# Images behind the first k, first parts of Q and K read straight from PSUM, second parts on ScalarE

## The chip, the cores and the metric

The kernel is one program on one core of one Trainium2 chip. The metric is the device time of one execution in microseconds (us). Engines are called as the profile calls them: PE (TensorE), DVE (VectorE), ACT (ScalarE), POOL (GpSimd), SP (SyncE, which here only issues transfers).

## The reference, cut to what matters

Two layers over `x` (2 batches, 512 tokens, 128 channels). Layer 0 scales `x` by a softmax over the batch and puts it through a ternary-weight feed-forward. Layer 1 is an attention over words with one image key in front (causal, 16 heads of 8), then a second attention without a mask, layer norm, a router that picks one of 8 experts, the experts, and a second layer norm.

```
x  = x + ffn0(cond0(x))                        # quantised feed-forward
c  = proj(softmax(q k' / sqrt(8) + causal) v)  # keys: one image key, 512 words
a  = out(softmax(q2 k2' / sqrt(8)) v2)         # second attention, no mask
h  = layernorm(c + a);  x = x + layernorm(h + moe(h))
```

## The kernel before

There are four attention instances `a`: 0 and 1 are the causal attention of batch 0 and 1, 2 and 3 the second attention of batch 0 and 1. An instance has 64 `scores` steps (16 heads by 4 row tiles: the score block is made only for its row maximum), two `max` steps (8 heads each), 32 `attend` steps (transposed scores of one head and half of the keys on PE, Exp on ACT), 16 `values` steps, 4 `turn_back` and `normalise` steps.

Q and K go into the score matmuls as three bf16 parts each, stacked along the contraction. A part is made by rounding, the next by rounding what is left. In step `q`, ACT reads the PSUM bank `misc` into `Qf` (line 733), waits for that, and copies `Qf` into `Qp[:, 0]` (line 736); `k` does the same with `Kf` and `Kp` (739, 742). In step `q_parts` DVE subtracts (953, `qres`), copies the residue to bf16 (954) and subtracts once more (956); `k_parts` is the same (960, 961, 963). In step `send` SP writes the parts to DRAM, q first and then k (517, 523), and reads them back as stacks in three ranges of heads: heads 0 to 3, 4 to 7, 8 to 15, for each `Qs` (529) and then `Ks` (535). SP waits in order, so no stack is read before the last k part was made.

When a `max` step is done, PE transposes the negated maxima (`max_rows`, line 1266), ACT copies them (745) and SP writes them as two more rows of `Qs` (540, "the shift"). `attend` 0 of an instance waits for the shift of heads 0 to 7, `attend` 16 for that of heads 8 to 15 (line 1271).

The order of all work is a string, `MERGE`: every letter takes the next step of one chain, and each engine runs its own share of the steps in that one order. So one letter moved changes the order on every engine that has work in its step. The steps of the text: `U` is `images` (PE: four small fp32 products with the image vector and biases, 1159 to 1169, into `s0`, and a fused weight, 1173, into `s1`; DVE reads `s0`, 908 to 912; ACT reads `s1`, 721). `w` is the turning of weights and then `prepare` (888 to 903). `S` is `stacks` twice (POOL memsets) and then `load_small` (nine POOL-issued loads, 609). `f` and `g` hold the feed-forward and then q, k, v of instances 0 and 1. There is one PSUM bank `misc`; its users take turns, each waiting until the last one was read.

Of the kernel before, what the change touches and what calls it, by code (L numbers as in the profile page):

```python
# [24 lines left out]
HD = D // HEADS  # L25
# [20 lines left out]
MERGE = (  # L46
    "ffwTfgfffwgffffffffwugUgfgff44ggggggggvSV4S00000000000000000000000000000g0000000mi0000g000m000g0"
    "00f50A0AAE0A050Ag0AA500FAA00a00i000a1a1mM1aA1Am1A111a11A1A1A1A11aaI11AA1M1aa1A1A11a11IAA1a1A1A1A"
    "1M1a1a1A1aimA11AaIA11AmA11a1A1Ma11aa1B11aI11Ba11B1q1B11qB661Bq1BBbGb11B1B1i11B1bBm2b6NB2m22B22B2"
    "2bJB22b22b22B2b2B2B2bN2B22B2B2b2B2B2B2bbJ22B2B2b2B2BN2b2B2Bm2B2Jb2b2b2m222bb22JNb22Cb22CC22r22C7"  # L50
    "r27C27crcC2C22C22C2OcH22mcC3C33C3m3C3C3c33c3C3C3cC3C3cK33c3OC3C3c33KCC3c3C3C33C3c33c3C33C3C3Ocm3"
    "C3m3lC3C3c33c3C3cD33cDK33cO3D3DcK3D3dSD33c3DD33n33QQnddDdPD3D3dLD33Dn3D3DmnDQmdQexddDdPDnDeDnDDd"
    "QDLxddDDyzDLDPddDzDdDdDDyPxdddeLdedxszyxseyRezxRyzesyesxzxRRzyesxyzxesyRozexyoezxzyeyxezxyzexyey"
    "zxzzpoppy"
)


def program_order():
# [42 lines left out]
    for a in range(INST):  # L101
        chains["0123"[a]] = each("scores", a, HEADS * NT)
        chains["4567"[a]] = [(n, a, 0) for n in ("q_parts", "k_parts", "send")]
        chains["EFGH"[a]] = [("v_bias", a, 0)]
        chains["ABCD"[a]] = each("attend", a, UNITS)
        chains["abcd"[a]] = output(a)
        chains["MNOP"[a]] = each("keep", a, ROUNDS)
        chains["IJKL"[a]] = each("normalise", a, ROUNDS)
# [93 lines left out]
def two_layers(nc, A, out):  # L202
# [18 lines left out]
    with ctx:  # L221
# [189 lines left out]
        r2_ready = sem("r2_ready")  # L411
        qhi_ready, khi_ready = sem("qhi_ready"), sem("khi_ready")
        qrest_ready, krest_ready = sem("qrest_ready"), sem("krest_ready")
# [33 lines left out]
        def _(sp):  # L447
            for step, a, i in ORDER:
# [52 lines left out]
                if step == "send":  # L501
# [9 lines left out]
                    for n in range(PARTS):  # L511
                        if n == 0:
                            sp.wait_ge(qhi_ready, a + 1)
                        else:
                            sp.wait_ge(qrest_ready, a * (PARTS - 1) + n)
                        for copy in range(n, 2 * PARTS - 1, PARTS):
                            sp.dma_start(dram_q[copy], Qp[:, n, :]).then_inc(parts_q[a], 16)
                    for n in range(PARTS):
                        if n == 0:
                            sp.wait_ge(khi_ready, a + 1)  # L520
                        else:
                            sp.wait_ge(krest_ready, a * (PARTS - 1) + n)
                        sp.dma_start(dram_k[n], Kp[:, n, :]).then_inc(parts_k[a], 16)
# [125 lines left out]
        def _(act):  # L649
# [4 lines left out]
            for step, a, i in ORDER:  # L654
# [71 lines left out]
                if step == "q":  # L726
                    if a >= 1:
# [4 lines left out]
                    ps = take("misc", "q", a)  # L732
                    act.activation(Qf[:, b, :], ps[:, :], ACT.Identity, bias=cols5[:, 0:1] if a < 2 else bjoin[:, 0:1],
                                   scale=float(HD) ** -0.5).then_inc(free["misc"], 1)
                    act.wait_ge(free["misc"], filled("misc", "q", a))
                    act.activation(Qp[:, 0, :], Qf[:, b, :], ACT.Copy).then_inc(qhi_ready, 1)
                if step == "k":
                    ps = take("misc", "k", a)
                    act.activation(Kf[:, :], ps[:, :], ACT.Identity,
                                   bias=cols5[:, 1:2] if a < 2 else bjoin[:, 1:2]).then_inc(free["misc"], 1)  # L740
                    act.wait_ge(free["misc"], filled("misc", "k", a))
                    act.activation(Kp[:, 0, :], Kf[:, :], ACT.Copy).then_inc(khi_ready, 1)
                if step == "max_rows":
# [42 lines left out]
        def _(dve):  # L786
# [50 lines left out]
            for step, a, i in ORDER:  # L837
# [103 lines left out]
                if step == "x1":  # L941
# [7 lines left out]
                    last.then_inc(free["pv"], 1)  # L949
                if step == "q_parts":  # L950

                    dve.wait_ge(qhi_ready, a + 1)
                    then_wait(dve.tensor_tensor(qres[:, :], Qf[:, b, :], Qp[:, 0, :], ALU.subtract))
                    dve.tensor_copy(Qp[:, 1, :], qres[:, :]).then_inc(qrest_ready, 1)
                    dve.wait_ge(qrest_ready, a * (PARTS - 1) + 1)
                    dve.tensor_tensor(Qp[:, 2, :], qres[:, :], Qp[:, 1, :], ALU.subtract).then_inc(qrest_ready, 1)
                if step == "k_parts":

                    dve.wait_ge(khi_ready, a + 1)
                    then_wait(dve.tensor_tensor(kres[:, :], Kf[:, :], Kp[:, 0, :], ALU.subtract))  # L960
                    dve.tensor_copy(Kp[:, 1, :], kres[:, :]).then_inc(krest_ready, 1)
                    dve.wait_ge(krest_ready, a * (PARTS - 1) + 1)
# [145 lines left out]
        def _(pe):  # L1108
# [6 lines left out]
            for step, a, i in ORDER:  # L1115
# [166 lines left out]
                if step == "values":  # L1282

                    r, kb = i // NT, i % NT
                    u = kb // 2
                    half = 2 * (a * ROUNDS + r) + u
                    ps = put("pv", "values", a, r) if kb == 0 else place["pv"]
                    if kb % 2 == 0:
# [119 lines left out]
```

## Time and profile before

| what | value |
|---|---|
| median of 3 runs | 357.32 us (356.76 to 358.71) |
| profiled execution, its own time | 352.93 us |
| its span, first to last instruction | 351.1 us |
| PE busy | 293.8 us (84%) |
| DVE busy | 258.8 us (74%) |
| ACT busy | 168.8 us (48%) |
| POOL busy | 29.3 us (8%) |
| mean granted clock | 0.96 |

The busy times are of the profiled execution, and the shares are of its span. PE and DVE take turns as the engine that others wait for; ACT has room over the whole span.

### The profile page before, as it was taken

What the parts mean: (1) busy time and instruction counts of PE and PEld (TensorE: products, weight loads), DVE (VectorE), ACT (ScalarE), POOL (GpSimd) and SP (SyncE); (2) the same over time, 40 slices, a digit from 0 to 9 for tenths busy, and PEclk for the clock granted to TensorE, in tenths of its full rate; (3) what the DMA queues carried; (4) which work ended last, traced back from release to release, by engine and by line L of the source; (5) the groups of instructions that cost most, each with busy time, mean ns of one, the idle gap of its engine ahead of it and who ended that gap; (6) DMA issues with size and microseconds to landing.
All of it is one profiled execution on the core that took longest, in us unless ns stands there. A gap on an engine that the chain in (4) does not pass through costs nothing.

```text
span 351.1 us, 5408 instructions
## 1 busy us (share of the span) xinstructions
PE 293.8 (84%) x1862; PEld 149.9 (43%) x1888; DVE 258.8 (74%) x764; ACT 168.8 (48%) x246; POOL 29.3 (8%) x58
## 2 busy tenths in 40 slices
PE   0286945988889999789999999999899999899981
PEld 0134531345445554244342332334334457656760
DVE  6888687999767788979999788777813128558445
ACT  1864360055555686166286676674767621221110
POOL 3075000000000000600000000003000001001001
PEclk9999686599999999999999999999999999999997
DMA  6892157214620027800037500260000000001001
GB/s 191 177 194 57 27 158 175 58 34 141 166 57 3 2 74 200 156 7 2 2 86 189 130 1 0 56 187 2 0 2 2 0 2 1 2 0 30 0 2 31
DMA packets 14959, 22.83 MB, mean 65 GB/s; under 512 B 2190, under 2 KB 12306, under 8 KB 14164
## 3 DMA queue, kind: packets, MB, share of 16 engines
q1 hardware_dynamic: 14644, 22.21, 25.7%
q0 software_dynamic: 288, 0.28, 0.7%
q8 instruction: 15, 0.25, 0.3%
q14 instruction: 12, 0.10, 0.1%
HBM read 13.99 MB, written 4.72 MB: 53 GB/s over the span
## 4 chain that ended last, share of the span: by engine, by line
PE 43%; DVE 22%; issue 14%; DMA 10%; ACT 6%; SPq 2%; POOL 1%; POOLq 0%; another core or an unknown queue 0%; DVEq 0%; ACTq 0%
PE ps_pv L1294 10%; DVE mx L989 9%; PE ps_t L1276 7%; PE ps_s L1253 6%; DMA Qs<-nmT 6%; PE ps_s L1369 5%; PE ps_misc L1377 4%; ACT probs L770 3%; DVE shared L985 2%; DMA shared<-in_L_ffn_w_down 2%; DVE probs L919 1%; DVE shared L833 1%; DVE q L922 1%; DVE mx L985 1%; DMA Ks<-parts_k 1%
## 5 line engine op out<-in xcount | busy, mean ns | idle before, releaser
L770 ACT ACTIVATE probs<-ps_t 128x1024 f32<-128x1024 f32 (+2 forms) x128 | 105.6, 862 | 61.8 <-PE ps_t L1279 26.4
L989 DVE TENSOR_REDUCE mx<-ps_s 128x1 f32<-128x512 f32 x126 | 80.8, 685 | 13.7 <-PE ps_s L1253 12.4
L1253 PE MATMUL ps_s<-Ks,Qs 128*128 128x512 bf16 (+3 forms) x220 | 70.6, 347 | 11.0 <-DVE mx L985 2.8
L1276 PE MATMUL ps_t<-Qs,Ks 128*128 128x512 bf16 (+3 forms) x245 | 65.4, 338 | 6.2 <-DMA Qs<-nmT 3.8
L1294 PE MATMUL ps_pv<-probs,Vs 128*32 128x512 f32 (+3 forms) x512 | 55.5, 522 | 0.3 <-ACT probs L770 0.2
L985 DVE CUSTOM_DVE_ANT_0 shared<-ps_s,shared 128x128 bf16<-128x128 f32 (+3 forms) x106 | 45.6, 459 | 10.4 <-PE ps_s L1253 9.5
L1253 PEld LDWEIGHTS ps_s<-Ks,Qs 128*128 128x128 bf16 x232 | 21.7, 98 | 57.9 <-DVE mx L989 26.8
L1093 DVE SCALAR_TENSOR_TENSOR shared<-ps_misc,comb,shared 128x128 f32<-128x128 f32 x64 | 18.0, 343 | 31.1 <-PE ps_misc L1377 31.1
L1276 PEld LDWEIGHTS ps_t<-Qs,Ks 128*128 128x128 bf16 x256 | 23.5, 98 | 32.4 <-issue 10.7
L1377 PE MATMUL ps_misc<-Ks,shared 128*128 128x128 f32 x256 | 31.6, 277 | 4.2 <-DVE shared L1093 1.4
L1377 PEld LDWEIGHTS ps_misc<-Ks,shared 128*128 128x128 f32 x256 | 30.5, 192 | 9.6 <-issue 8.2
L1369 PE MATMUL ps_s<-Qf,Ks 128*128 128x512 f32 x64 | 30.3, 596 | 0.0
L756 ACT ACTIVATE shared<-ps_s,cols 128x512 f32<-128x512 f32 x16 | 11.0, 686 | 36.7 <-PE ps_s L1369 36.7
L1279 PE MATMUL ps_t<-causal_k,identb 128*128 128x128 bf16 x128 | 24.5, 219 | 0.3 <-issue 0.2
L1294 PEld LDWEIGHTS ps_pv<-probs,Vs 128*32 128x32 f32 x512 | 11.4, 108 | 21.2 <-issue 20.0
L639 POOL TENSOR_TENSOR shared<-shared,halves 128x4 f32<-128x4 f32 x4 | 4.1, 1036 | 193.7 <-DVE shared L823 193.7
L753 ACT ACTIVATE shared<-ps_pv 128x512 f32<-128x512 f32 x16 | 9.6, 597 | 12.1 <-PE ps_pv L1294 12.0
L1369 PEld LDWEIGHTS ps_s<-Qf,Ks 128*128 128x128 f32 x64 | 11.0, 191 | 9.5 <-issue 9.0
L1084 DVE TENSOR_SCALAR shared<-ps_s,cols 128x512 f32<-128x512 f32 x16 | 11.9, 744 | 3.4 <-PE ps_s L1369 3.4
L1279 PEld LDWEIGHTS ps_t<-causal_k,identb 128*128 128x128 bf16 x128 | 12.5, 98 | 3.2 <-issue 0.3
L985 DVE CUSTOM_DVE_ANT_0 shared<-ps_t,shared 128x512 bf16<-128x512 f32 (+1 forms) x22 | 13.0, 626 | 0.0
L633 POOL TENSOR_TENSOR Zimg<-Vimg,Pimg 128x288 f32<-128x288 f32 x4 | 2.7, 682 | 107.6 <-ACT Pimg L750 107.6
(244 smaller groups left out, 324.2 us busy)
## 6 DMA issues: line engine op xcount, KB each, us to landing
parts_q<-Qp SPq DMA_DIRECT2D x20, 128.0 KB, 1.9
Qs<-parts_q SPq DMA_DIRECT2D x24, 96.0 KB
Ks<-parts_k SPq DMA_DIRECT2D x24, 96.0 KB
Qs<-parts_q SPq DMA_DIRECT2D x12, 192.0 KB
Ks<-parts_k SPq DMA_DIRECT2D x12, 192.0 KB
Ks<-Qs SPq DMA_DIRECT2D x2, 1024.0 KB, 12.0
parts_k<-Kp SPq DMA_DIRECT2D x12, 128.0 KB, 1.8
Qs<-Qs SPq DMA_DIRECT2D x1, 1024.0 KB, 12.2
```

What stands on the lines that cost most here:

```text
L756: act.activation(hid[:, i % 2, 1, :], ps[:, :], ACT.Relu, bias=cols17[:, 2 * i + 1:2 * i + 2])\
L770: act.activation(probs[:, half % 2, j, 0:w], ps[:, 0:w], ACT.Exp).then_inc(free[f"t{i % 2}"], 1)
L985: last = dve.tensor_tensor_reduce(out=added[:, n % 2, 0:w], in0=ps[:, 0:w], in1=causal_q[:, S - w:], scale=1.0, scalar=LEAST, op0=ALU.add, ...
L989: last = dve.tensor_reduce(mx[:, b, t, h:h + 1], ps[:, 0:w], AX, ALU.max)
L1084: dve.tensor_scalar(hid[:, i % 2, 0, :], ps[:, :], cols17[:, 2 * i:2 * i + 1], 0.0, ALU.add, ALU.max).then_inc(free["s0"], 1)
L1093: last = dve.scalar_tensor_tensor(out=acc[:, a, t, :], in0=ps[:, t * D:(t + 1) * D], scalar=comb[:, a, t, i // 2, i % 2:i % 2 + 1], in1=ac ...
L1253: mm = pe.matmul(ps[:, 0:w], Qs[:, b, h, t * P:(t + 1) * P], Ks[:, b, h, 0:w], start=True, stop=True)
L1276: mm = pe.matmul(ps[:, col:col + w], Ks[:, b, h, kb * P:(kb + 1) * P], Qs[:, b, h, S - w:S], start=True, stop=(a >= 2))
L1279: mm = pe.matmul(ps[:, col:col + P], identb[:, :], causal_k[:, :], start=False, stop=True)
L1294: mm = pe.matmul(ps[j * HC:(j + 1) * HC, S - w:S], Vs[:, b, kb, r * GROUP + j, :], probs[:, half % 2, j, col:col + w], start=(kb == 0), st ...
L1369: pe.matmul(ps[:, :], W1[:, i, h * P:(h + 1) * P], X3T[:, a, :], start=True, stop=True)\
L1377: mm = pe.matmul(ps[:, t * D:(t + 1) * D], hid[:, i % 2, h, t * P:(t + 1) * P], W2[:, i, h, :], start=(h == 0), stop=(h == FH - 1))
```

## The change

1. `MERGE` is a new string. On PE and ACT `images` stands behind the first `q` and `k` of instance 0 (before: ahead of the last two `ffn_up` of batch 1); on DVE it stands between `q_lo` and `k_lo` of instance 0. `prepare` stands three steps earlier. `load_small` on POOL stands before the first `max_rows` (before: behind the fourth). In the attention stages `scores`, `attend` and `values` are merged anew: `attend` 16 of instance 0 stands behind `scores` 11 of instance 1 and ahead of `values` 4 (before: behind `scores` 16 and `values` 5).
2. `Qp[:, 0]` and `Kp[:, 0]` are read from PSUM with bias and scale, without a wait between the two reads. The bank is free after the second read.
3. The second parts are made by ACT (steps `q_mid`, `k_mid`) in place of DVE.
4. The subtractions are the DVE steps `q_res`, `k_res`, `q_lo`, `k_lo`, which other steps can stand between.
5. `values` 0 waits for the step that writes `Vs`.

```diff
-        chains["4567"[a]] = [(n, a, 0) for n in ("q_parts", "k_parts", "send")]
+        chains["4567"[a]] = [(n, a, 0) for n in ("q_res", "q_mid", "k_res", "k_mid", "q_lo", "k_lo", "send")]
...
                     act.activation(Qf[:, b, :], ps[:, :], ACT.Identity, bias=cols5[:, 0:1] if a < 2 else bjoin[:, 0:1],
+                                   scale=float(HD) ** -0.5)
+                    act.activation(Qp[:, 0, :], ps[:, :], ACT.Identity,
+                                   bias=cols5[:, 0:1] if a < 2 else bjoin[:, 0:1],
                                    scale=float(HD) ** -0.5).then_inc(free["misc"], 1)
-                    act.wait_ge(free["misc"], filled("misc", "q", a))
-                    act.activation(Qp[:, 0, :], Qf[:, b, :], ACT.Copy).then_inc(qhi_ready, 1)
...
+                if step == "q_mid":
+                    act.wait_ge(qres_ready, a + 1)
+                    act.activation(Qp[:, 1, :], qres[:, :], ACT.Copy).then_inc(qrest_ready, 1)
+                if step == "k_mid":
+                    act.wait_ge(kres_ready, a + 1)
+                    act.activation(Kp[:, 1, :], kres[:, :], ACT.Copy).then_inc(krest_ready, 1)
...
-                if step == "q_parts":
-
-                    dve.wait_ge(qhi_ready, a + 1)
-                    then_wait(dve.tensor_tensor(qres[:, :], Qf[:, b, :], Qp[:, 0, :], ALU.subtract))
-                    dve.tensor_copy(Qp[:, 1, :], qres[:, :]).then_inc(qrest_ready, 1)
+                if step == "q_res":
+                    dve.wait_ge(free["misc"], filled("misc", "q", a))
+                    dve.tensor_tensor(qres[:, :], Qf[:, b, :], Qp[:, 0, :], ALU.subtract).then_inc(qres_ready, 1)
+                if step == "k_res":
+                    dve.wait_ge(free["misc"], filled("misc", "k", a))
+                    dve.tensor_tensor(kres[:, :], Kf[:, :], Kp[:, 0, :], ALU.subtract).then_inc(kres_ready, 1)
+                if step == "q_lo":
                     dve.wait_ge(qrest_ready, a * (PARTS - 1) + 1)
                     dve.tensor_tensor(Qp[:, 2, :], qres[:, :], Qp[:, 1, :], ALU.subtract).then_inc(qrest_ready, 1)
-                if step == "k_parts":
...
+                if step == "k_lo":
                     dve.wait_ge(krest_ready, a * (PARTS - 1) + 1)
                     dve.tensor_tensor(Kp[:, 2, :], kres[:, :], Kp[:, 1, :], ALU.subtract).then_inc(krest_ready, 1)
...
+                    if i == 0:
+                        pe.wait_ge(free["misc"], filled("misc", "v", a))
```

The two strings, taken apart into PE's steps of instances 0 and 1 around `attend` 16 (`sc` scores, `at` attend, `va` values, `tb` turn_back, `mr` max_rows):

```
before: mr0.1 sc1.4 at11 sc1.5-7 tb0.0 sc1.8-9 at12 sc1.10 at13 sc1.11 at14 sc1.12 at15 sc1.13-14
        va0.4-5 sc1.15-16 at16-17 sc1.17-18 va0.6-7
after:  mr0.1 sc1.3 at11 sc1.4 at12 sc1.5-6 tb0.0 sc1.7 at13 sc1.8 at14 sc1.9-10 at15 sc1.11 at16
        sc1.12 va0.4 sc1.13-14 va0.5-6 sc1.15 at17
```

DVE's steps of instance 0 at the front:

```
before: down0.3 prepare x1.0 ffn_up1.1 images ffn_up1.2-3 q_parts k_parts r2t1.0 ...
after:  (prepare behind r2t0.0) down0.3 x1.0 ffn_up1.1-3 q_res k_res q_lo images k_lo r2t1.0 ...
```

## Rows read from the trace of the kernel before

**Rows 1.** The page: busy time, granted clock in 40 slices, a group of scores on DVE.
```profile
PE 293.8 (84%) x1862; PEld 149.9 (43%) x1888; DVE 258.8 (74%) x764; ACT 168.8 (48%) x246; POOL 29.3 (8%) x58
PEclk9999686599999999999999999999999999999997
...
L985 DVE CUSTOM_DVE_ANT_0 shared<-ps_s,shared 128x128 bf16<-128x128 f32 (+3 forms) x106 | 45.6, 459 | 10.4 <-PE ps_s L1253 9.5
```

**Rows 2.** The chain that ended last, 28 to 100 us: start, us, what.
```profile
34.58 0.22 PE ps_s L1159 x2
...
38.26 1.49 PE ps_s L1173 x2
...
83.93 2.08 DMA parts_k<-Kp
...
95.44 6.07 DMA Qs<-nmT
```

**Rows 3.** Timeline, 33.5 to 62 us: start, duration, engine, line, operation, count, idle before.
```profile
35.23 1.12 DVE L946 SCALAR_TENSOR_TENSOR X<-ps_pv,q,X 128x128 f32<-128x128 f32 x4
...
38.29 0.49 DVE L908 COPY Vimg<-ps_s 128x128 f32<-128x128 f32 x2 [0.63 <-PE ps_s L1169]
...
43.87 0.69 ACT L733 ACTIVATE Qf<-ps_misc,cols 128x512 f32<-128x512 f32 x1 [0.84 <-PE ps_misc L1229]
...
44.59 0.63 ACT L736 ACTIVATE Qp<-Qf 128x512 bf16<-128x512 f32 x1
44.61 1.12 PE L1233 MATMUL ps_misc<-XT,Wcaq 128*128 128x512 f32 x2 [0.84 <-ACT Qf L733]
...
46.32 0.43 DVE L954 CAST Qp<-qres 128x512 bf16<-128x512 f32 x1
...
48.57 0.69 DVE L963 TENSOR_TENSOR Kp<-kres,Kp 128x512 bf16<-128x512 f32 x1
...
55.91 0.29 DVE L985 CUSTOM_DVE_ANT_0 shared<-ps_s,shared 128x128 bf16<-128x128 f32 x1 [1.22 <-PE ps_s L1253]
```

**Rows 4.** Windows of 2 us: busy us per engine, granted clock, DMA share, GB/s.
```profile
38.00:40.00 2.00, 2.00 (x6) 0.93 (x6) 0.94 (x5) 0.22 (x1) 0.00 (x0) 0.50 0.19 25
...
44.00:46.00 2.00, 1.12 (x2) 0.30 (x2) 1.83 (x8) 1.41 (x3) 0.00 (x0) 1.00 0.02 4
```

**Rows 5.** SP's own timeline of DMA issues, 44 us to the end.
```profile
84.30 1.45 SPq L529 DMA_DIRECT2D Qs<-parts_q  x3
...
132.92 1.21 SPq L529 DMA_DIRECT2D Qs<-parts_q  x3
...
139.10 1.19 SPq L535 DMA_DIRECT2D Ks<-parts_k  x3
140.63 32.59 SPq L540 DMA_DIRECT2D Qs<-nmT  x4
...
191.65 1.18 SPq L535 DMA_DIRECT2D Ks<-parts_k  x3
```

**Rows 6.** PE's timeline at the waits for the shift of heads 8 to 15.
```profile
98.49 1.71 PE L1294 MATMUL ps_pv<-probs,Vs 128*32 128x512 f32 x16
...
101.56 0.39 PE L1276 MATMUL ps_t<-Qs,Ks 128*128 128x512 bf16 x1 [0.98 <-DMA Qs<-nmT]
...
150.32 0.39 PE L1276 MATMUL ps_t<-Qs,Ks 128*128 128x512 bf16 x1 [2.55 <-DMA Qs<-nmT]
...
151.13 0.64 PE L1294 MATMUL ps_pv<-probs,Vs 128*32 128x256 f32 x8
...
201.22 0.61 PE L1276 MATMUL ps_t<-Qs,Ks 128*128 128x512 bf16 x2 [0.30 <-DMA Qs<-nmT]
```

**Rows 7.** POOL's timeline: the first and the last of the nine loads.
```profile
141.43 0.78 POOL L609 DMA_DIRECT2D Wr<-in_L_ffn_w_group  x1
...
146.18 0.54 POOL L609 DMA_DIRECT2D norm_gb<-in_L_ffn_ln_b  x1
```

**Rows 8.** Windows of 10 us: busy us per engine, granted clock, DMA share, GB/s.
```profile
130.00:140.00 10.00, 9.94 (x90) 5.58 (x91) 8.82 (x30) 6.52 (x11) 0.00 (x0) 1.00 0.75 209
```

More of the change, by code:

```diff
@@ L46 @@
 MERGE = (
[L47 to L54, printed above, removed]
+    "ffwTfffgfwgfwfffffffuVggfgff44444U4ggggggggv0S0000000000000000000000000SS400g00000000mi0000g0000"
+    "m000g0050055AA05fA5005A0A0AAE00a00Ag0AF00aMa0a1i5Am1A1m1A1A11a1A1A11A1A1Ia11aa1A1MA1a1A1a11A1A1a"
+    "11AI1aA1A1A11aa1AA1M1mi1A1AmA1A1aM11a1Ia1a1aIB11aBBa11B1q11B11Bq611b666BB61q61b1bb1GB16B11B1B11N"
+    "imBB22Bm22B22b22b22b2b22B22B2BN2b2B22B2B2B2B2JBB22b2bN22b2b2b2BmBJ2mB2B2bJ2B2b2BN2b2bb2C2Jb2C2b2"
+    "C2r2C2C227r2277c722CC72cC722r2C222C72C2Hc2Cm33cO3m3C3C3c33c3CKC33c3C3CO3c33c3CC33c3C3C3c3C3C3c3C"
+    "3C33Kc33CC3Ocm33mCC33c3KC3c3C3c33cD3O3c3D3DK3c3Dc3D3D3n33n3QDDd33dDQdlP3dD3D3n3D3D3dDL33mDQneQmD"
+    "ddexDnDQdDdDPnDDdDdDdDDyDDdPdLDDdDxdzDdLyzPddexdedLsyxzxsRzexRzyexyzesyxRzeRszyyesseyexoRxzyxzxe"
+    "yzexyeooyzxzexzxyzzpeppyy"
 )
@@ L411, in two_layers @@
         r2_ready = sem("r2_ready")
-        qhi_ready, khi_ready = sem("qhi_ready"), sem("khi_ready")
+        qres_ready, kres_ready = sem("qres_ready"), sem("kres_ready")
         qrest_ready, krest_ready = sem("qrest_ready"), sem("krest_ready")
@@ L512, in _ @@
                         if n == 0:
-                            sp.wait_ge(qhi_ready, a + 1)
+                            sp.wait_ge(free["misc"], filled("misc", "q", a))
                         else:
@@ L519, in _ @@
                         if n == 0:
-                            sp.wait_ge(khi_ready, a + 1)
+                            sp.wait_ge(free["misc"], filled("misc", "k", a))
                         else:
@@ L739, in _ @@
                     act.activation(Kf[:, :], ps[:, :], ACT.Identity,
+                                   bias=cols5[:, 1:2] if a < 2 else bjoin[:, 1:2])
+                    act.activation(Kp[:, 0, :], ps[:, :], ACT.Identity,
                                    bias=cols5[:, 1:2] if a < 2 else bjoin[:, 1:2]).then_inc(free["misc"], 1)
-                    act.wait_ge(free["misc"], filled("misc", "k", a))
-                    act.activation(Kp[:, 0, :], Kf[:, :], ACT.Copy).then_inc(khi_ready, 1)
+                if step == "q_mid":
[4 more added lines that the diff above has]
+                    act.activation(Kp[:, 1, :], kres[:, :], ACT.Copy).then_inc(krest_ready, 1)
                 if step == "max_rows":
@@ L949, in _ @@
                     last.then_inc(free["pv"], 1)
-                if step == "q_parts":
-                    dve.wait_ge(qhi_ready, a + 1)
-                    then_wait(dve.tensor_tensor(qres[:, :], Qf[:, b, :], Qp[:, 0, :], ALU.subtract))
-                    dve.tensor_copy(Qp[:, 1, :], qres[:, :]).then_inc(qrest_ready, 1)
+                if step == "q_res":
[5 more added lines that the diff above has]
+                if step == "q_lo":
                     dve.wait_ge(qrest_ready, a * (PARTS - 1) + 1)
                     dve.tensor_tensor(Qp[:, 2, :], qres[:, :], Qp[:, 1, :], ALU.subtract).then_inc(qrest_ready, 1)
-                if step == "k_parts":
-                    dve.wait_ge(khi_ready, a + 1)
-                    then_wait(dve.tensor_tensor(kres[:, :], Kf[:, :], Kp[:, 0, :], ALU.subtract))
-                    dve.tensor_copy(Kp[:, 1, :], kres[:, :]).then_inc(krest_ready, 1)
+                if step == "k_lo":
                     dve.wait_ge(krest_ready, a * (PARTS - 1) + 1)
```

## The prediction

> **What bounds the kernel now.** I read the page first. PE is busy for 84% of the span, DVE for 74%, ACT for 48% [rows 1]. A bound by one engine would show one of them near 100% everywhere, so the next view was busy time by windows. From 110 us on PE is nearly full (9.94 of 10 us between 130 and 140, where DVE has 8.82) [rows 8]; ahead of that no engine is. So a microsecond is to be won in two ways: an earlier start of the attention, or a shorter idle of PE behind 100 us. The chain of waits names both places. In the front it runs over PE's `images` (34.58 to 39.75) [rows 2], the first q and k, their parts, and the trip of the stacks through DRAM. DVE takes the first score at 55.91, 6.65 us after the last k part was made at 49.26 [rows 3]. Behind 80 us it runs over the second trip (the last k part written from 83.93 on) and over the shift, whose transfer takes 6.07 us and ends at 101.51 [rows 2]. PE's timeline shows what the shifts cost: it sits idle for 0.98 us ahead of 101.56, 2.55 ahead of 150.32 and 0.30 ahead of 201.22 [rows 6]. SP's timeline tells why they are long: each is issued behind the eighteen stack reads of the next instance, and lands only when those are through [rows 5].
>
> The change touches both places. I take it in order of time; "earlier" and "later" are against the trace of before.
>
> **The front.** `images` goes from ahead of the first q to behind the first k. Its 5.2 us of PE [rows 2] leave the way of q, but not all of it is won. `x1` ends at 36.35 [rows 3] and cannot come earlier: `prepare` is moved ahead of it, which costs DVE as much there, and the wait for PE's last `down` product is no longer covered; I put it 0.5 later. Behind it stand the turning of x, one `ffn_up` and q, at the lower clock: the granted clock was 0.50 (1.2 GHz) between 38 and 40 and 1.00 (2.4 GHz) between 44 and 46 [rows 4], and PE had been little busy before it fell. Counting these from the end of `x1` I get ACT's first read of q at 40.9 in place of 43.87 [rows 3]: 3.0 earlier.
> The k product waited for one read of the bank (0.69) and now for two; the second takes the place of the 0.63 copy and was hidden behind PE's product [rows 3]. That takes 0.7 back: the k product ends at 43.5, 2.2 earlier than 45.73.
> The last k part then needs 0.69 + 0.69 for the two reads, the ACT copies of q and k (0.63 each) and the last subtraction: it could end at 46.9. But on DVE `images` stands ahead of `k_lo`. PE needs from 34.58 to about 38.26 for the part that DVE reads, some 3.7 us with half of it at the lower clock [rows 2], 2.9 if all of it runs at the higher; DVE's three kinds of reads then take 0.49 and about 0.6 more [rows 3], 1.05. So `k_lo` starts at 43.5 + 2.9 + 1.05 = 47.5 and ends at 48.2, 1.1 earlier than before (49.26); at the lower clock it ends 0.2 earlier. I take **1.0 earlier**, ends 0.2 and 2.3 (`images` not in the way). SP waits for `k_lo` before it reads any stack, so the first score follows as before, at 54.9. The fused weight (1.49 us) [rows 2] and ACT's copy of it delay the start of batch 1's turn by 0.4 at most, with 1.22 us of DVE idle ahead of the first score [rows 3] to cover it.
>
> **Parts of instance 1.** Between the residue of q and the last part of k, DVE loses two casts (0.43 each) [rows 3] and the 0.69 of the V bias, which now stands behind, and takes one more score of 256 columns, 0.4 (the mean of a score is 0.46) [rows 1]: 1.2 less. `k_mid` sits on ACT behind two Exps and is done just in time. I take **1.1 earlier**, ends 0.3 (an Exp late) and 1.2. The stack reads, issued from 84.30 [rows 5], start 2.1 earlier with the front's share, and as the shift lands 17.2 us after their start, it lands at 99.4.
>
> **What PE has to do meanwhile.** This is the part that speaks against the change. Before, PE does scores up to 16 and `values` 4 and 5 ahead of `attend` 16 and still idles for 0.98. Now five scores and two `values` stand behind it. The two `values` are 1.71 us [rows 6]; the scores have 1408 columns, 0.6 us at 2.4 GHz. So 2.3 us of PE work is pushed behind the wait, which grows to about 3.8, and PE has 9.94 of 10 us behind it [rows 8], so it isn't caught up. Cost **2.3 later**, ends 0 (if PE's 1.3 us of idle in the 20 us behind it, and the longer wait, take it in) and 2.3. Sum so far: -1.0 - 1.1 + 2.3 = 0.2 later.
>
> **Instance 2.** Ahead of its k stand three scores fewer and two `attend` more, 0.2 us of PE. Its k product goes to the last part in 1.12 + 0.69 + 0.69 for the bank, then three subtractions and a score of 0.6: 5.2 against 4.65 (44.61 to 49.26) [rows 3], as the parts now pass through ACT and DVE with a score between. 0.6 later. So the stacks start 1.0 later. Against that, `load_small` is gone from there. Its nine loads were issued from 141.43 to 146.72 [rows 7], just while the shift waited behind the stacks. From the end of the last stack issue to the wait's end took 150.32 - 140.29 = 10.0 us there, and 201.22 - 192.83 = 8.4 at the next instance, with the same stacks and no such loads [rows 5, 6]. I take **1.5 earlier**, ends 0 and 1.6. At its new place, about 31 to 37 us, the DMA share was low (0.19 at 38 us) [rows 4]. One `values` (0.55 of PE) [rows 6] moves ahead of the wait and one score behind it, 0.3 earlier. At 150 us the balance is 0.2 + 0.2 + 0.6 - 1.5 - 0.3 = -0.8.
> The Trainium skill (DMA: Bandwidth & Descriptors, "Queues, rings and completion order") says that each DMA engine goes round its queue rows packet by packet. By that alone nine small loads would take only their own few packets from the shift, and the term would be near its end of 0; the whole sum below would then be 0.1 later instead of 1.4 earlier.
>
> **Instances 3 and the rest.** Its k stands four scores earlier, so the wait of 0.30 at 201.22 [rows 6] goes. Two casts fewer on a DVE that is about as full as PE there are worth 0.4 of their 0.86. The four ACT copies per pair (0.63) [rows 3] fall to an engine at 48% [rows 1] and are hidden behind PE's scores and the two `attend` results that lie ready; without that cover they cost 0.6 an instance. In the experts, `y` 7 of batch 0 stands right behind `y` 6, which shows DVE's add to PE, and one step later a stall goes: 0.1 later. Added wait for `Vs`: its writer ends before PE comes, 0. Together -0.6.
>
> **Sum:** -0.8 - 0.6 = -1.4. The profiled span was 351.1 with 1.8 us around it; I forecast a span of 349.7. The median shown, 357.32, is 4.4 above the profiled execution's 352.93, and I carry the difference over: **355.9 us**.
>
> **Rivals.**
> *The waits are worth more than I count (faster).* For it: PE's idle behind 100 us is where a full engine loses, and all three waits shrink or move. If the pushed work is taken in by the wait at 150 (its end hangs on DMA alone, not on PE) and only 1.0 of the 2.3 stays, the sum is -2.7, and with the casts in full -3.2: 354.1 to 354.6. Against it: the stacks that set the wait at 150 start when PE reaches k of instance 2, so the push moves that as well.
> *DVE's backlog (the other side, slower).* At `attend` 16 DVE has done five scores fewer, 2.6 us with reading the sum (0.46 the mean, and 0.08). DVE must catch up before instance 2's first scores, in a stretch where it is busy for 8.82 of 10 us [rows 8] and has 1.2 to spare; there it gets three scores more between k and `attend` 16. If PE waits for it, up to 2.6 + 1.5 come on top: +2.7, 360.0. It decides from 3.2 us of such waits on (then the sum is over 1.8). For it: every score bank waits for DVE. Against it: 100 to 120 us has room on DVE.
> *The change does nothing in the front.* `images` only changes places with k. If PE's clock is at its lower level behind q (PE idles 1.5 us between q and k, during the two reads), `k_lo` ends only 0.2 earlier: the sum is -0.6, 356.7. The Trainium skill (TensorE: Matmul & The Clock Gate, Part 1) says that the throttled level is the default and activity releases it, which would give this case; the row at 44 us, 1.00 with PE busy for 1.12 of 2 us [rows 4], speaks against it.
>
> **Chances.** 0.5% is 1.8 us, about what a measurement of this kernel can tell from no change. My forecast (between -2.2 and -0.8) 0.35; more than that won 0.30; nothing in the front or the loads worth nothing (-0.8 to +1.0) 0.17; DVE's backlog or the push in full 0.18. The forecast's case lies across the bound, so a third of it counts as faster: faster 0.42, within 0.5% 0.40, slower 0.18. The bad ends of all terms together give +2.1, so the range ends at 359.3; all the good ones together would give -5.8, but that needs them all, and I cut the range at -4.3: 353.0.
>
> **What the next profile would show.** ACT's first read of q near 41, k's product behind it, `images` ending near 46.5, `k_lo` behind DVE's reads of `s0`, first score at 54.9. Stacks of instance 1 from 82.2; PE idle for some 4 us ahead of `attend` 16, which starts at 99.5. Stacks of instance 2 from 134, wait's end near 149.8. I am wrong if the idle at `attend` 16 is under 2 us, if the shift at 150 still needs 10 us from the last stack issue, or if DVE releases PE's scores for more than 2 us in total beyond before between 110 and 145.

## The result, and the profile after

The changed kernel takes 360.11 us, median of 20 runs (355.84 to 367.74), against 356.64 for the kernel before on the same chips, also 20 runs (352.44 to 361.86). The ratio is 1.016, with a 95% interval of 1.0118 to 1.0201; timed once more, beside other kernels, it was 1.0116 (1.0049 to 1.0182). I had forecast 355.9 with a range of 353.0 to 359.3, and called slower the least likely of the three. It came out slower.

These ratios leave out runs more than 1.5% above a kernel's fastest one, so where a kernel scatters widely I also give the ratio of the medians over all runs, with an interval from resampling them. For the changed kernel the medians give 1.0097 (1.0012 to 1.0176), and in the second timing 0.9975 (0.995 to 1.009). So by the medians the loss is 3.5 us in the first timing and can't be told from nothing in the second; what the change does inside the kernel is read from the traces below.

The page of the changed kernel (busy time, granted clock in 40 slices, a group of scores on DVE), against [rows 1]:

```profile
PE 293.4 (82%) x1862; PEld 149.8 (42%) x1888; DVE 253.8 (71%) x756; ACT 173.2 (49%) x254; POOL 29.0 (8%) x58
PEclk9995885699989999989999999999999999999997
...
L990 DVE CUSTOM_DVE_ANT_0 shared<-ps_s,shared 128x512 bf16<-128x512 f32 (+3 forms) x107 | 46.6, 462 | 14.5 <-PE ps_s L1258 12.9
```

The casts did go from DVE (5.0 us less) to ACT (4.4 more). PE has the same work and a longer span, 356.3 against 351.1. So what was lost is idle time of PE, with a slower clock in places (mean 0.946 against 0.96), and PE's own rows show where.

The front, in the timeline of all engines (start, duration, engine, line, operation, count, idle before), against [rows 3]:

```profile
40.38 0.69 ACT L733 ACTIVATE Qf<-ps_misc,cols 128x512 f32<-128x512 f32 x1 [0.61 <-PE ps_misc L1234]
40.96 0.68 ACT L735 ACTIVATE Qp<-ps_misc,cols 128x512 bf16<-128x512 f32 x1
...
41.69 1.13 PE L1238 MATMUL ps_misc<-XT,Wcaq 128*128 128x512 f32 x2 [1.42 <-ACT Qp L735]
...
46.09 0.28 DVE L917 COPY vbias<-ps_s 128x128 f32<-128x128 f32 x1
46.29 0.33 DVE L919 TENSOR_SCALAR bjoin<-ps_s,cols 128x1 f32<-128x1 f32 x2
...
46.54 0.68 DVE L968 TENSOR_TENSOR Kp<-kres,Kp 128x512 bf16<-128x512 f32 x1
...
53.52 0.29 DVE L990 CUSTOM_DVE_ANT_0 shared<-ps_s,shared 128x128 bf16<-128x128 f32 x1 [0.27 <-PE ps_s L1258]
```

ACT reads q 3.5 us earlier (43.87 before), the last k part stands behind DVE's reads for `images`, as forecast, and ends at 47.22 in place of 49.26, and the first score comes 2.4 earlier. The front was worth more than I said: 2.4 us for 1.0.

PE at the three waits for the shift, and SP's issues (the row of `zrow`, L505, is the first thing SP does for the next instance; the first stack read and the shift of that instance follow it), against [rows 5, 6]:

```profile
99.02 0.53 PE L1281 MATMUL ps_t<-Qs,Ks 128*128 128x512 bf16 x1 [3.51 <-DMA Qs<-nmT]
...
100.12 1.94 PE L1301 MATMUL ps_pv<-probs,Vs 128*32 128x512 f32 x8
...
152.57 0.39 PE L1281 MATMUL ps_t<-Qs,Ks 128*128 128x512 bf16 x1 [2.88 <-DMA Qs<-nmT]
...
206.45 0.60 PE L1281 MATMUL ps_t<-Qs,Ks 128*128 128x512 bf16 x2 [2.03 <-DMA Qs<-nmT]
```

```profile
81.64 1.20 SPq L529 DMA_DIRECT2D Qs<-parts_q  x3
...
127.37 0.84 SPq L505 DMA_DIRECT2D Qs<-zrow  x1
...
135.82 1.24 SPq L529 DMA_DIRECT2D Qs<-parts_q  x3
...
143.26 28.60 SPq L540 DMA_DIRECT2D Qs<-nmT  x4
...
180.06 0.79 SPq L505 DMA_DIRECT2D Qs<-zrow  x1
...
190.31 1.24 SPq L529 DMA_DIRECT2D Qs<-parts_q  x3
```

The first wait ends 2.5 us earlier than before, the second 2.25 later. 4.8 us are lost between the two, 4.2 of them ahead of L505 (125.73 before, by the same row). Windows of 2 us (busy time per engine, granted clock, DMA share, GB/s) show a part of it that I had not reckoned with:

```profile
96.00:98.00 2.00, 0.00 (x0) 0.00 (x0) 0.24 (x2) 0.00 (x0) 0.00 (x0) 1.00 0.38 89
98.00:100.00 2.00, 0.98 (x5) 0.51 (x5) 0.00 (x0) 0.00 (x0) 0.00 (x0) 0.78 0.00 1
100.00:102.00 2.00, 2.00 (x11) 0.22 (x10) 1.06 (x5) 0.00 (x0) 0.00 (x0) 0.50 0.00 0
102.00:104.00 2.00, 1.90 (x22) 0.64 (x20) 0.91 (x4) 0.46 (x1) 0.00 (x0) 0.86 0.00 0
```

PE does nothing between 96 and 98, and then its granted clock falls to 0.50 (1.2 GHz), just as it has work again: eight matmuls of `values` take 1.94 us. In the kernel before the same windows read 1.00. The Trainium skill (TensorE: Matmul & The Clock Gate, Part 1) says that activity releases the throttled level; the 1.00 of the busy windows agrees, and these rows show the clock lost again in the middle of a kernel.

The same happens behind the second wait, in the changed kernel's windows (first two rows) and not in those of the kernel before (last two; its wait ends at 150.32):

```profile
152.00:154.00 2.00, 1.43 (x9) 0.84 (x10) 0.51 (x1) 0.67 (x1) 0.00 (x0) 0.94 0.00 0
154.00:156.00 2.00, 2.00 (x8) 0.73 (x6) 1.47 (x3) 1.32 (x3) 0.00 (x0) 0.50 0.00 0
...
152.00:154.00 2.00, 1.86 (x19) 0.95 (x19) 1.84 (x3) 1.38 (x2) 0.00 (x0) 1.00 0.00 0
154.00:156.00 2.00, 1.86 (x12) 0.94 (x12) 1.99 (x4) 1.91 (x4) 0.00 (x0) 1.00 0.00 0
```

### The profile page after: what moved, and what is told of

It reads as the page before. It is cut to its first block, busy times and chain, and to the rows that moved or that the text cites. A ratio compares the mean times of both kernels' runs of the same rounds, so it can differ in the third digit from the quotient of the medians.

```text
span 356.3 us, 5412 instructions
## 1 busy us (share of the span) xinstructions
PE 293.4 (82%) x1862; PEld 149.8 (42%) x1888; DVE 253.8 (71%) x756; ACT 173.2 (49%) x254; POOL 29.0 (8%) x58
## 4 chain that ended last, share of the span: by engine, by line
PE 48%; issue 16%; DVE 15%; DMA 9%; ACT 7%; SPq 3%; POOLq 0%; POOL 0%; DVEq 0%; ACTq 0%
PE ps_pv L1301 12%; PE ps_t L1281 8%; PE ps_s L1258 7%; DMA Qs<-nmT 6%; PE ps_misc L1384 4%; PE ps_s L1376 4%; DVE mx L994 3%; ACT probs L777 2%; DVE shared L990 2%; DMA shared<-in_L_ffn_w_down 2%; PE ps_misc L1234 1%; DVE probs L926 1%; SPq L535 1%; PE ps_t L1284 1%; DMA parts_k<-Kp 1%
## 5 line engine op out<-in xcount | busy, mean ns | idle before, releaser
L994 DVE TENSOR_REDUCE mx<-ps_s 128x1 f32<-128x512 f32 x128 | 82.6, 686 | 17.3 <-PE ps_s L1258 15.1
L1281 PE MATMUL ps_t<-Qs,Ks 128*128 128x512 bf16 (+3 forms) x249 | 66.6, 343 | 11.3 <-DMA Qs<-nmT 8.4
L1301 PE MATMUL ps_pv<-probs,Vs 128*32 128x512 f32 (+3 forms) x512 | 57.4, 532 | 0.8 <-DVE Vs L975 0.3
L990 DVE CUSTOM_DVE_ANT_0 shared<-ps_s,shared 128x512 bf16<-128x512 f32 (+3 forms) x107 | 46.6, 462 | 14.5 <-PE ps_s L1258 12.9
L1258 PEld LDWEIGHTS ps_s<-Ks,Qs 128*128 128x128 bf16 x235 | 22.0, 99 | 60.6 <-DVE mx L994 28.3
L990 DVE CUSTOM_DVE_ANT_0 shared<-ps_t,shared 128x384 bf16<-128x384 f32 (+1 forms) x21 | 12.3, 617 | 0.1
```

Of the source, the lines that this page charges most:

```text
L990: last = dve.tensor_tensor_reduce(out=added[:, n % 2, 0:w], in0=ps[:, 0:w], in1=causal_q[:, S - w:], scale=1.0, scalar=LEAST, op0=ALU.add, ...
L994: last = dve.tensor_reduce(mx[:, b, t, h:h + 1], ps[:, 0:w], AX, ALU.max)
L1258: mm = pe.matmul(ps[:, 0:w], Qs[:, b, h, t * P:(t + 1) * P], Ks[:, b, h, 0:w], start=True, stop=True)
L1281: mm = pe.matmul(ps[:, col:col + w], Ks[:, b, h, kb * P:(kb + 1) * P], Qs[:, b, h, S - w:S], start=True, stop=(a >= 2))
L1301: mm = pe.matmul(ps[j * HC:(j + 1) * HC, S - w:S], Vs[:, b, kb, r * GROUP + j, :], probs[:, half % 2, j, col:col + w], start=(kb == 0), st ...
```

## The experiments

I had two theories. **A:** the new order loses the time. A1 is the place of `attend` 16 of instance 0, with the pushed work and the clock behind it; A2 is the longer way from q to the stack reads in instances 2 and 3. **B:** the new instructions lose it (two reads of PSUM, casts on ACT). Each run is read by its ratio to the kernel before on its own chip and by one stretch of its trace, from the end of the first shift wait to the end of the second, which starts behind the front and ends ahead of the rest. It is 48.76 us before and 53.55 in the changed kernel. Its first part, up to L505, is 24.17 and 28.35.

**1. `attend` 16 later, all else as changed.** One letter of the order moves; in steps:

```diff
-attend 15, attend 16, scores 12, values 4, scores 13-14, values 5-6, scores 15, attend 17
+attend 15, scores 12, values 4, scores 13-14, values 5-6, scores 15, attend 16, attend 17
```

> The changed kernel with one TensorE step moved: attend 16 of instance 0 behind scores 12 to 15 and values 4 to 6 of the same stretch. If that wait and the lower clock behind it cost time (theory A1): the idle there falls from 3.5 us to 1 us or less, the granted clock stays at 1.00 between 98 and 104 us, k of instance 2 is issued 2.5 to 4 us earlier and the time falls by 2 to 4 us. If the time is lost behind it, in the q and k chains of instances 2 and 3 alone (theory A2): the idle shrinks, but the time stays within 1 us of the changed kernel's.

The ratio is 1.0032 (0.998 to 1.0084). The wait ends at 98.92 with 0.68 of idle, the stretch is 49.31 and the span 351.8. Most of what the change lost is gone, as A1 says. PE's timeline of that run:

```profile
95.58 1.06 PE L1301 MATMUL ps_pv<-probs,Vs 128*32 128x512 f32 x8
...
98.92 0.39 PE L1281 MATMUL ps_t<-Qs,Ks 128*128 128x512 bf16 x1 [0.68 <-DMA Qs<-nmT]
```

The eight matmuls of `values` now run ahead of the wait, at the full clock (1.06 us).

**2. The same move backwards, in the kernel before.**

```diff
-attend 15, scores 13-14, values 4-5, scores 15-16, attend 16, attend 17
+attend 15, attend 16, scores 13-14, values 4-5, scores 15-16, attend 17
```

> The kernel before with one step of TensorE and ScalarE moved: attend 16 of instance 0, which waits for the first shift, stands directly behind attend 15, ahead of scores 13 to 16 and values 4 and 5 of the old order, near its place in the changed kernel. If that one place costs what the changed kernel lost there: the wait still ends at about 101.6, TensorE's idle before it rises from 0.98 to 3.5 or more, the granted clock falls behind it, and the span is 3.5 to 4.5 us longer (355). If only the pushed work counts (four scores and two values, 2.3 us): 353.4. If a longer wait costs nothing since the work is done in it later anyway: 351.1.

The kernel scattered from 353.5 to 368.1, so its ratio (0.9968, 0.9889 to 1.0047) rests on two of twelve runs and says little. The medians are 361.31 and 357.01: 1.012 (1.005 to 1.022). The first wait ends at 101.46 with 3.60 of idle, the second at 155.94; the stretch is 54.5, and from the wait's end to L505 it takes 28.61 in place of 24.17. The span of this execution, 359.0, is above the 355 that I expected, but those 4.4 us are what I expected of the place. One step put too early makes the kernel before lose the stretch in full, without any new instruction.

**3. The wait filled.** Fifteen products that nothing uses, in the PSUM place that `attend` 16 claims anyway and then overwrites:

```diff
+                    ps = put(f"t{i % 2}", "weights", a, i)
+                    if (a, i) == (0, UNITS // 2):
+                        for n in range(15):
+                            pe.matmul(ps[:, 0:S], identb[:, :], Ks[:, b, 0, :], start=True, stop=True)
                     if i % (UNITS // 2) == 0:
                         pe.wait_ge(shifted[a][i // (UNITS // 2)], 16 * 2)
```

> The changed kernel with 15 extra matmuls of 128x512 (about 3.2 us, their output is overwritten and used by nothing) between the claim of the PSUM place for attend 16 of instance 0 and its wait for the shift. If the fall of the clock behind the wait is due to TensorE's idle: granted clock 1.00 from 98 to 104, the values behind the wait take 1.1 instead of 1.94 us for eight, and the second wait ends 1.5 to 2 us earlier than in the changed kernel (from the first wait's end to the second's 51.7 instead of 53.6), ratio about 1.006 to 1.008. If the pushed work alone counts, or the clock falls anyway: 53.6 and 1.012.

The ratio is 1.0027 (0.9985 to 1.0069). PE's timeline and windows:

```profile
95.29 3.40 PE L1280 MATMUL ps_t<-Ks,identb 128*128 128x512 bf16 x15
99.01 0.39 PE L1284 MATMUL ps_t<-Qs,Ks 128*128 128x512 bf16 x1 [0.32 <-DMA Qs<-nmT]
...
99.66 1.06 PE L1304 MATMUL ps_pv<-probs,Vs 128*32 128x512 f32 x8
```

```profile
98.00:100.00 2.00, 1.68 (x13) 0.62 (x14) 0.24 (x3) 0.00 (x0) 0.00 (x0) 1.00 0.03 4
100.00:102.00 2.00, 2.00 (x26) 0.53 (x18) 1.74 (x9) 0.05 (x1) 0.00 (x0) 1.00 0.00 0
```

The wait ends where it did (99.01), no useful work is done earlier, and yet L505 comes at 125.78 in place of 127.37. The 1.6 us are the clock's. From the wait's end to L505 it now is 26.77, with `attend` 16 later 24.52: the pushed work is 2.25 us, the clock 1.6. The medians on one chip agree with the first figure: 356.42 here, 354.10 with `attend` 16 later (run 8). The ratio fell by more than 1.6 us against the changed kernel's, but that one wasn't measured beside it.

**4. q and k steps of instances 2 and 3 drawn together** (A2's remedy). For instance 3 (scores, attend and values are instance 2's):

```diff
-q, scores 46, attend 3, scores 47, attend 4, scores 48-49, q_res, k, scores 50-51, q_mid, k_res, values 0, k_mid, scores 52-53, ...
+q, scores 46, attend 3, scores 47, q_res, k, q_mid, scores 48, k_res, k_mid, q_lo, k_lo, attend 4, scores 49-51, values 0, scores 52-53, ...
```

> The changed kernel with the q and k steps of instances 2 and 3 drawn together: k one attend and two to three scores earlier, no scores between k_res, q_lo and k_lo, no Exp between k and k_mid. Theory A2 (these chains set the stack reads, and with them the waits at 152.6 and 206.5 us): stack reads of instance 3 start 2 to 4 us earlier, the wait at 206.5 us (2.0 us idle) goes, and the time falls by 2 to 4 us. Theory A1: at most 1 us, since TensorE comes late to both places anyway.

The ratio is 1.026 (1.0184 to 1.0337), worse. The reads of instance 3 are issued at 189.43 in place of 190.31, 0.9 earlier where A2 wanted 2 to 4. But the chain goes from DVE to ACT and back twice, and DVE works in order: with next to no scores between, it stands in those waits, and PE with it.

```profile
130.59 1.13 PE L1238 MATMUL ps_misc<-shared,Wjoin 128*128 128x512 f32 x2 [0.99 <-ACT Qp L735]
...
135.79 0.28 PE L1258 MATMUL ps_s<-Ks,Qs 128*128 128x256 bf16 x1 [3.03 <-DVE mx L990]
```

The scores come late, with them the maxima, and SP issues the shifts of nmT at 147.56 and 204.40 (143.26 and 198.67 in the changed kernel). The scores in between are the cover of these waits.

**5. The old order with the new code** (`q_res` and `q_mid` at the place of `q_parts`, the other four at that of `k_parts`), no change of the order otherwise.

> The order of the kernel before, with the new instructions: the two reads from PSUM, the second parts on ScalarE, the subtractions where q_parts and k_parts stood. Theory A (the loss comes from the new order): time within 0.5% of before or a little faster, and the stack reads of instances 2 and 3 within 0.7 us of 132.9 and 185.5. Theory B (the loss comes from the new instructions, ScalarE's two copies more being late for the last k part): about as slow as the changed kernel, +1.0 to +1.6%, with the stack reads of instance 3 at 188 us or later.

The ratio is 1.0297 (1.0235 to 1.0359). ACT's timeline in instance 1:

```profile
83.52 3.40 ACT L777 ACTIVATE probs<-ps_t 128x896 f32<-128x896 f32 x4 [0.23 <-PE ps_t L1284]
87.00 0.63 ACT L749 ACTIVATE Kp<-kres 128x512 bf16<-128x512 f32 x1
```

The cast of k stands behind four Exps, DVE's last subtraction waits for it, and the stack reads of instance 1 go out at 89.70 in place of 84.30. So the new code needs the new order, and this run doesn't separate the two.

**6. The new order with the old code.** The parts stand all on DVE in one step each, at the places of `q_res` and `k_res`; the added wait for `Vs`, which the new order needs, is kept.

> The changed kernel's order with the old code of the parts: first part copied from Qf or Kf on ScalarE, residue, middle part and third part all on VectorE in one step, placed where the new order has q_res and k_res; TensorE's added wait for the values kept. If the loss comes from the order (attend 16 too early, q and k spread out) it stays: span 355 to 357. The old step holds VectorE for its whole length at the place of q_res, so the stacks of instances 2 and 3 would be read earlier than in the changed kernel by the two trips to ScalarE, by 1 to 3 us (134 and 188). If the loss comes from the new instructions, the span goes back to 351.

The ratio is 0.9947 (0.9899 to 0.9994). In the profile PE is idle for 2.96 ahead of `attend` 16 and the stretch is 52.9, like the changed kernel's, so A's sign is there without any new instruction. But the median (355.04 against 357.01) doesn't show that loss, and that B would have said. From L505 to the first stack read it takes 7.74 us in instance 2 and 9.22 in instance 3; 8.45 and 10.25 in the changed kernel.

**7. The same with `attend` 16 later**, by the step diff of run 1, on two chips.

> The old code of the parts in the changed kernel's order, with attend 16 of instance 0 moved behind scores 12 to 15 and values 4 to 6. The same move took 1.4 us off the changed kernel's distance to the kernel before by the medians, and 4.5 off its profiled span; the old code in the new order stood 2.0 us under the kernel before. If the two add up: 3.5 to 6 us below the kernel before, ratio 0.984 to 0.990. If the move was worth nothing without the new code (one cause counted twice): 0.9945, as without it.

> The changed order with attend 16 later and the old code of the parts everywhere, once more, on this chip. If it beats the kernel before beyond doubt: ratio 0.985 to 0.992 again. If the new code in instances 0 and 1 costs nothing, it equals a16_later_old_code_2_3.

The ratios are 0.9911 (0.9866 to 0.9955) and 0.9968 (0.9933 to 1.0003), the spans 350.2 and 351.1. One interval lies below 1, the other just touches it. In both profiles the shift has landed before PE comes to `attend` 16. With the next run's mixed version it is the fastest with the new order throughout.

**8. Where the new code costs.** On one chip with the second of these: `attend` 16 later with the new code everywhere, and with the old code in instances 2 and 3.

```diff
-                if step == "k_res":
+                if step == "k_res" and a >= 2:
+                    dve.wait_ge(khi_ready, a + 1 - 2)
+                    then_wait(dve.tensor_tensor(kres[:, :], Kf[:, :], Kp[:, 0, :], ALU.subtract))
+                    dve.tensor_copy(Kp[:, 1, :], kres[:, :]).then_inc(krest_ready, 1)
...
+                if step == "k_res" and a < 2:
```

> The changed kernel with attend 16 of instance 0 later, once more, for a comparison on one chip with the two below. Ratio 1.003, first to second wait 49.3 us.

> The same with the old code of the parts for instances 2 and 3. If the new code's cost is the longer way to the stack reads there (0.7 and 1.1 us): 1.8 us under attend16_later_again, ratio 0.998. If it costs in instances 0 and 1, or elsewhere, 1.003 as that one. L505 to first stack read 7.7 and 9.2 instead of 8.4 and 10.2.

The ratios are 0.9989 (0.9953 to 1.0025) and 0.994 (0.99 to 0.998); old code everywhere was 0.9968. Between the three there is at most 0.5%, and not in the order that B would give. The reads move as expected (7.75 and 9.22 from L505). A cost of the new instructions of one or two us isn't excluded, and isn't shown either.

The first of the two shows something unexpected. PE stood idle for only 1.32 ahead of `attend` 16, and the clock fell all the same, behind the wait's end at 99.47:

```profile
98.00:100.00 2.00, 0.68 (x6) 0.35 (x6) 0.70 (x2) 0.00 (x0) 0.00 (x0) 1.00 0.04 10
100.00:102.00 2.00, 1.48 (x12) 0.83 (x10) 0.30 (x2) 1.73 (x2) 0.00 (x0) 0.85 0.00 0
102.00:104.00 2.00, 2.00 (x15) 0.75 (x14) 0.99 (x4) 0.96 (x2) 0.00 (x0) 0.50 0.00 0
```

The stretch was 52.05 there, against 49.31 without the fall. Of these 2.7 us 1.45 lie ahead of L505 (25.97 for 24.52), where the clock fell; 1.2 are a slower shift behind it (10.02 us from its issue for 8.85).

**9. The same in the changed kernel with `attend` 16 early** (old code in instances 2 and 3).

> The changed kernel with the old code of the parts (all on VectorE, in one piece, at the places of q_res and k_res) for instances 2 and 3, and the new code for 0 and 1. If the new code costs where its casts go to ScalarE and come back while scores and Exps stand between, in instances 2 and 3: the stack reads come 0.7 and 1.1 us earlier than in the changed kernel from the row before them (L505 to first stack read 8.45 and 10.25 there, 7.7 and 9.2 with the old code), the ratio falls from 1.010 to 0.995 or so by medians. If the cost is in instances 0 and 1, the ratio stays at 1.010 and more.

The ratio is 1.0054 (1.0003 to 1.0104), against 1.0116 for the changed kernel beside it; by all medians 0.999 and 0.9975, so there is no difference that can be told. In this one execution the shift took 9.3 us from its issue (92.24) to the wait's end (101.58), PE stood idle for 6.17, and the stretch was 54.0.

**10. `load_small` put back** behind `max_rows` of instance 1.

> The changed kernel with one step put back: load_small of instance 2 stands behind max_rows of instance 1 again, as before. My prediction gave its move 1.5 us at the second shift's wait; the changed kernel's trace bears out 0.6 (last stack issue to the wait's end 10.0 before, 9.4 after), and that might be chance. If the move is worth what I said: the second wait ends at 154.1 instead of 152.57 and the span is 357.8 or more. If it is worth 0.6: 153.2, span 356.9, a ratio that can't be told from the changed kernel's. If it is worth nothing, 152.6 and 356.3.

The ratio is 1.0158 (1.008 to 1.0237), as the changed kernel's. The second wait ends at 152.93; from the issue of the shift (143.51) that is 9.42 us, with the loads moved 9.31 and, again, 8.84. The move is worth 0.1 to 0.6 us. All profiles together say the same: 8.9 to 9.8 us with the loads there (six), 8.2 to 10.0 without them (ten).

**11. The front alone:** old code, the new order up to the first scores, the old order behind.

```diff
-r2t 0-1, ..., down 2-3, prepare, x1, ffn_up 1, images, ffn_up 2, x1t, ffn_up 3, q, k, q_parts, k_parts
+r2t 0, prepare, r2t 1, ..., down 2-3, x1, fixed_rows, ffn_up 1-2, x1t, ffn_up 3, q, k, q_parts, k_parts, images
```

> The old code, in the changed kernel's order up to the first scores of instance 0 (images and prepare behind the first k) and in the old order from there on. If the gain at the front (first score 2.4 us earlier, of which old code keeps perhaps 1.5 to 2) is carried to the end: span 349.1 to 349.6, ratio 0.995. If the shift and stack waits swallow it: 351.1.

The ratio is 0.9908 (0.9856 to 0.996). The first score comes at 53.98, 1.9 earlier, and the stretch is 48.5. The times say that the gain is carried to the end. The profile doesn't show it on the way: the stack reads of instance 1 go out 0.7 earlier (83.58), the first wait ends 0.1 earlier (101.42), and this execution's span is 355.4. The granted clock was 0.83 between 70 and 80 us there and 0.98 in the first profile of the kernel before.

**12. Both kernels once more**, for how far one execution stands for its kernel.

> The kernel before, once more, as the measure of how far one profiled execution stands for the kernel. By medians 1.000 within 0.004. Its profiled span of 351.1 was 3.5 under the median of its runs less 1.8. Kernels with the same order behind the second shift took 53.2 to 53.9 us from the second shift wait's end to the third's, and the kernel before's profile 50.9: if that was this one execution's luck, the second profile shows 53 or more; if it is the kernel's own, 51.

> The changed kernel once more, beside the others on one chip. By medians 1.010 (3.5 us above the kernel before), the wait before attend 16 of instance 0 idles TensorE for 3.5 us, and the granted clock falls behind it, if both are the kernel's and not one execution's. If the fall of the clock is chance, it may stay at 1.00 here, and the second wait comes 1.8 us earlier than 152.6.

The ratios are 0.9993 (0.9952 to 1.0034) and 1.0116 (1.0049 to 1.0182); the medians are 357.52 and 357.91, of the kernel before beside them (33 runs) 358.79. The kernel before had a span of 356.1 this time, 5.0 more than in its first profile. The windows of 10 us show where part of it went:

```profile
60.00:70.00 10.00, 9.04 (x29) 3.34 (x28) 10.00 (x47) 0.52 (x1) 0.00 (x0) 0.50 0.45 99
70.00:80.00 10.00, 9.25 (x32) 4.69 (x31) 7.90 (x39) 3.34 (x6) 0.00 (x0) 0.55 0.01 2
```

From 70 to 80 the clock was 0.55 here, 0.98 in the first profile; the first score came 1.5 later and the stack reads of instance 1 went out 3.5 later, at 87.83. Another 1.7 lie behind the third wait. But its stretch was 48.05, and the changed kernel's second one 54.17, each near that of its first profile.

All profiles in which the stretch can be read, with its first part, from the wait's end to L505:

| `attend` 16 | clock behind it | stretch, us | to L505, us |
|---|---|---|---|
| late, old order | stays | 48.76, 48.05, 48.5 | 24.17, 24.17, 24.17 |
| late, new order | stays | 49.31 | 24.52 |
| late, new order | falls | 52.05 | 25.97 |
| early, wait filled | stays | 52.02 | 26.77 |
| early, old order | falls | 54.5 | 28.61 |
| early, new order | falls | 53.55, 54.17, 53.67, 52.9, 54.0 | 28.35, 29.47, 28.30, 28.36, 29.51 |

The two figures over 29 are those of the longest idles, 4.75 and 6.17 us.

## Why the prediction was wrong

By its own stretches, between the two first profiles:

| stretch | forecast | measured |
|---|---|---|
| first wait's end | -2.1 | -2.5 |
| from there to L505 of instance 2 | +2.3 | +4.2 |
| from L505 to the second wait's end | -1.0 | +0.6 |
| from there to the end | -0.6 | +2.95; +1.0 by the means of all profiles |

**The front** was right in mechanism and undersized: 2.4 for 1.0 at the first score. PE ran the images at the full clock (1.00 from 42 to 46). **Instance 1's parts** were oversized: the stack reads came 2.66 earlier (81.64), so they added 0.3, not 1.1; the two errors nearly cancel in the first row. The rival "does nothing in the front" is refuted by run 11 as well.

**"What PE has to do meanwhile" is the step that failed.** It said: "2.3 us of PE work is pushed behind the wait ... Cost **2.3 later**, ends 0 ... and 2.3." The pushed work was 2.25 us (runs 1 and 3), so the estimate of the work was right, and PE did not catch up. But 2.3 stood as the upper end of the range, and the real cost was 3.9 to 4.2: I took a long wait to cost just its length. PE's idle of 3.5 us brings its clock down behind it, another 1.6 (run 3). I had read such falls in the front of the same trace [rows 4] and used them for the images, but not for a wait that my own working made four times as long. I had also misread them there: "PE had been little busy before it fell" holds for 26 to 30 us (0.67 and 0.39 of 2), but from 30 to 36 PE was busy for 1.82 to 1.92 of 2, and the clock fell only at 36 to 38 (0.55). None of my three signs of being wrong showed either: the idle was 3.51, the shift took 9.4 from the last stack issue, and DVE's maxima held PE for 0.6 us against 0.4 between 110 and 145. No sign looked at the clock.

**`load_small`** was the second wrong term: 1.5 forecast, at most 0.6 measured (run 10). I had compared the shift behind the stacks of instance 2, 10.0 us from the last stack issue, with the one behind those of instance 3, 8.4. But SP issues the first one directly behind the stacks (140.63) and the second 2.7 us after them (195.54, last stack issue over at 192.83), since its maxima were late. Counted from its own issue, the shift took 9.7 and 5.7. Over all profiles the one behind instance 3's stacks took 5.7 to 7.1 where it was issued 2.7 us or more after them and 7.3 to 8.4 where it was issued sooner. That fits less of the stacks' traffic left to meet, which no run isolates. The loads account for at most 0.6 of the difference. The Trainium skill (DMA: Bandwidth & Descriptors, "Queues, rings and completion order") gave the term its end near 0, and the measured size agrees with that end (9.42 us with the loads, 9.31 without); the turn-taking itself is in no row.

**Instances 2 and 3.** I had 0.6 for the longer chain of parts. From L505 to the first stack read it is 1.25 longer in instance 2 (7.19 to 8.45) and 1.95 in instance 3 (8.30 to 10.25). SP sends the q parts in order and can't send a k part before the last q part, which now stands behind scores. Yet old code there takes back 0.7 and 1.0 of this (runs 6, 8, 9) and the ratios show no gain beyond 0.5%, so at most 1.7 us are the longer chain's. The words "so the wait of 0.30 at 201.22 ... goes" were wrong: it was 2.03. From the second wait's end to the third's it took 50.90 and 51.50 in the kernel before, 53.88 and 55.04 in the changed one. By the test that I had set in run 12 (51 or 53) that is the kernels' own, and no luck of one execution. Part of it is the clock again. From the second wait's end to L505 of instance 3, six profiles with the new order and the fall behind that wait take 27.3 to 27.6 us, five with the new order and no fall 26.2; the old order takes 26.9 without the fall (both profiles of the kernel before) and 28.3 and 28.5 with it (runs 11 and 2). So this fall costs 1.1 to 1.6 us, and the new order itself gains 0.7 there. To the end of the kernel the spread is wider: 200.8 to 205.5, mean 203.1, in four profiles with the old order there, 203.2 to 205.7, mean 204.1, in six with the new order and code, mean 203.0 in five with old code in instances 2 and 3. So about 1 us is lost behind the second wait; how it divides between order and code is not shown.

**DVE's backlog**, my rival on the slower side, is refuted. Between 99 and 152 us PE waited 1.3 us for maxima, 0.6 before. The median, 360.11, landed where that rival had put it (360.0), by another mechanism; that is luck. My range, cut at 359.3, left out the price of my own rival.

**Sum.** -2.5 + 2.25 + 1.6 + 0.3 (the rest ahead of L505) + 0.6 = 2.25 later at the second wait, and about 1 more behind: 3.3 us, near the first timing's medians (3.5). The ratios are above that (1.016 is 5.7 us, 1.0116 is 4.1) and the second timing's medians below it (no loss). So the traces show where the loss arises, and the times leave its size between 0 and 6 us.

**Open:** why the old code in the new order loses less by `attend` 16's early place (run 6 against 7: 0.9947 to 0.9911 or 0.9968) than the new code does (1.0116 to 1.0032 or 0.9989). Its one profile shows the same stretch; more profiles of that kernel would be needed. As long as that is so, a part of the loss by B isn't excluded.

## What to carry to other kernels

When work in an in-order queue is put behind a wait for a transfer, count the pushed work in full, and add the clock: here 3.5 us of idle brought TensorE back at half its clock, for another 1.6 us. Look behind every long wait for the clock, not only where the change is. Put the step that waits as far back as its result allows, and compare transfers from their own issue, not from the end of something ahead of them. One profiled execution can differ from the next of the same kernel by 5 us; compare stretches between fixed events over several profiles before a difference is given a cause.

## What the runs showed of the hardware

The granted clock fell behind an idle of 3.51 us (0.50 between 100 and 102 us), and stayed at 1.00 when useless products filled the same wait. In all seven profiles with 2.96 to 6.17 us of idle ahead of `attend` 16 of instance 0 it fell. The length of the idle alone doesn't decide: over both waits it also fell behind 1.32 (PE busy for 0.68 of the 2 us around it), 1.69 and 2.40, and it stayed behind 1.96, 2.38 and 2.55. A fall cost 1.1 to 1.6 us at such a wait, and more behind the longest idles. Two reads of one PSUM bank by ACT stand 0.58 us apart (40.38 and 40.96) though each row lasts 0.69, so the second read costs 0.6 and not 0.7. The shift took from 5.7 to 10.0 us from its issue to the end of the wait, least where it was issued 2.7 us or more behind the last stack read.
